# Four edits to a fused two-layer kernel: feed-forward weights loaded in the layer ahead, held-back expert loads, a reordered first tap in the scan, and another order of the scan's last projection

## The reference

```python
x = x + 0.5 * experts(layernorm(x))       # 8 experts, best 2 per token: silu(x@w1[e]) * (x@w3[e]) @ w2[e]
x = x + attention(layernorm(x))           # 32 heads of width 8, rotary positions
x = x + 0.5 * experts(layernorm(x))       # the same weights again
x = x + 0.5 * sparse_ffn(layernorm(x))    # silu(x@gate) * (x@up), best 2 of every 4 kept, @ down
x = x + state_space_scan(layernorm(x))    # 32 heads of 128: conv of 4 taps, silu, chunked scan, gate, norm, @ out_proj
x = x + 0.5 * sparse_ffn(layernorm(x))    # the same weights again
```

## Time and profile before

| | |
|---|---|
| three runs | 1654.58, 1649.94, 1653.99 us; median 1653.99 |
| profiled execution | 1655.48 us; span 1653.7 us, so 1.8 us lie around it |
| PE busy | 1437.4 us (87%), mean granted clock 0.939 |
| DVE / ACT / POOL busy | 1139.2 (69%) / 878.2 (53%) / 497.1 us (30%) |
| first expert layer | from 10.8 us |
| second expert layer | from 607.0 us |
| first feed-forward | from 775.7 us |
| scan heads | 980 to 1547 us |
| second feed-forward | 1548.6 to 1647 us |

### The profile page before, as it was taken

One profiled execution on the slowest core, in us unless ns is written; L12 is line 12 of the kernel. 1 busy time (PEld: TensorE's weight loads), 2 busy tenths in 40 slices (PEclk: granted clock), 3 DMA queues, 4 the chain that ended last, 5 costly groups with the idle time before them and its releaser, 6 DMA issues. The chain is left out here.

```text
span 1653.7 us, 25033 instructions
## 1 busy us (share of the span) xinstructions
PE 1437.4 (87%) x7896; PEld 1056.5 (64%) x7896; DVE 1139.2 (69%) x2026; ACT 878.2 (53%) x1238; POOL 497.1 (30%) x407
## 2 busy tenths in 40 slices
PE   3999489999999966994997968899999999998697
PEld 3788343333333345883786757788887887887586
DVE  5622599989989847332775756777776777867475
ACT  2422227767767744322434765667575665755332
POOL 1444210000000113542001114655645556564100
PEclk9999759999999977997997998999999999999899
DMA  8532211111111028334001103222322222221200
GB/s 296 146 52 46 58 31 21 23 25 20 27 28 27 5 96 286 52 52 120 2 0 40 42 25 91 83 90 90 96 77 85 77 96 90 84 90 39 77 1 26
DMA packets 83030, 112.06 MB, mean 68 GB/s; under 512 B 11905, under 2 KB 60801, under 8 KB 82913
## 3 DMA queue, kind: packets, MB, share of 16 engines
q1 hardware_dynamic: 73152, 96.05, 19.5%
q0 software_dynamic: 9376, 14.16, 4.8%
q10 hardware_dynamic: 384, 0.39, 0.1%
HBM read 89.99 MB, written 11.93 MB: 62 GB/s over the span
## 5 line engine op out<-in xcount | busy, mean ns | idle before, releaser
L962 DVE TENSOR_REDUCE attn_max_chunks<-attn_scores 128x1 f32<-128x512 f32 x488 | 305.4, 684 | 30.7 <-PE attn_scores L1213 25.2
L1124 ACT ACTIVATE attn_probs<-attn_scoresT 128x1024 f32<-128x1024 f32 x256 | 248.2, 1022 | 118.8 <-PE attn_scoresT L1229 118.6
L1213 PE MATMUL attn_scores<-attn_k_picks,attn_q_group 64*128 64x512 f32 x488 | 188.5, 466 | 14.5 <-DVE attn_max_chunks L962 6.0
L1213 PEld LDWEIGHTS attn_scores<-attn_k_picks,attn_q_group 64*128 64x128 f32 x488 | 85.7, 191 | 178.5 <-DVE attn_max_chunks L962 170.4
L1644 DVE SCALAR_TENSOR_TENSOR ssm_scan_x<-ssm_scan_proj,ssm_w_conv,ssm_scan_x 128x1023 f32<-128x1023 f32 (+2 forms) x96 | 123.1, 1282 | 84.1 <-ACT ssm_scan_x L1639 78.4
L1229 PE MATMUL attn_scoresT<-attn_q_group,attn_k_picks 64*128 64x512 f32 x512 | 153.9, 438 | 3.3 <-ACT attn_probs L1124 3.3
L1241 PE MATMUL attn_o<-attn_probs,attn_v_group 128*32 128x512 f32 x1024 | 139.2, 616 | 0.4 <-ACT attn_probs L1124 0.3
L62 PE MATMUL ssm_scan_proj<-ssm_xnT_hi,ssm_w_in_hi 128*128 128x512 f32 x256 | 111.0, 434 | 27.8 <-DVE ssm_scan_x L1644 22.5
L293 POOL DMA_INDIRECT moe_sums<-moe_xn,moe_token x46 | 77.7, 1690 | 128.4 <-DVE moe_xn L430 122.6
L2481 PE MATMUL ssm_scan_out<-ssm_scan_w_out,ssm_scan_v 128*128 128x256 f32 x480 | 110.7, 384 | 4.6 <-POOL ssm_scan_w_out L2186 4.4
L481 ACT ACTIVATE moe_xnT<-moe_gate 128x512 f32<-128x512 f32 x46 | 27.5, 597 | 153.6 <-PE moe_gate L64 153.6
(11 more groups left out here) (355 smaller groups left out, 3400.5 us busy)
## 6 DMA issues: line engine op xcount, KB each, us to landing
ssm_cum_all<-ssm_cums SPq DMA_DIRECT2D x32, 512.0 KB, 3.7
ssm_scan_exp_cum<-ssm_cums SPq DMA_DIRECT2D x32, 512.0 KB, 3.7
moe_w_gate_lo<-in_moe_w SPq DMA_DIRECT2D x16, 512.0 KB, 11.2
moe_w_up_lo<-in_moe_w SPq DMA_DIRECT2D x16, 512.0 KB, 11.1
moe_w_down<-in_moe_w SPq DMA_DIRECT2D x16, 512.0 KB, 11.1
ssm_w_in<-in_in_w SPq DMA_DIRECT2D x64, 128.0 KB, 2.6
ssm_scan_w_out<-in_out_w SPq DMA_DIRECT2D x8, 512.0 KB, 3.8
moe_sums<-main_residual SPq DMA_DIRECT2D x2, 1024.0 KB, 5.6
```

The source lines that it names most:

```text
L962: return nc.vector.tensor_reduce(rmaxc[:, half, place:place + 1], chunk_bank(g, n), AX_X, ALU.max).then_inc(reduced, 1)
L1124: nc.scalar.activation(probs[s % 2][:, 2 * pair:2 * pair + 2, :], st_ps[pair][:], ACT.Exp, scale=SCALE).then_inc(exp_done, 1)
L1213: nc.tensor.matmul(chunk_bank(g, n), qs[b][head_rows(j), t * P:(t + 1) * P], kz[b][head_rows(j), j % 2, c * BANK:(c + 1) * BANK], start=Tr ...
```

## The change

Four edits. (1) A buffer `ffn.room` of 32 KB a partition lives from the second expert layer to the end. In that layer it is `w_down`; when the last `down` product is done, SP loads the feed-forward's gate and up weights into it and waits for them, and only then waits for the scatter-adds and reloads `xres`. In the scan it holds `cT` and `cum_all`, and behind the last `cgrow` SP loads the same weights again. `sparse_ffn_layer` no longer loads them; ACT casts the first half of gate ahead of the first tokens, DVE subtracts for the first half of gate and the second of up, POOL for the other two. (2) In both expert layers SP holds back the loads of experts 4 to 7 until the first gather has landed; the casts of expert 0 come ahead of the router's tanh on ACT and its first subtraction ahead of the router on DVE; the others follow the first `low_x`; gate and up wait for their own parts, `down` for its own transfer. (3) In the scan ACT makes `tap(n+1)` before `square(n-1)`. (4) The last `w_out` goes into the buffer of `grow`, so that its load waits for `cgrow` alone; PE projects the first three heads of two pairs ahead of the last head's v, then adds the fourth, and `norm_sums` writes to the bank of y.

```diff
+SPLIT_AHEAD = 2
+LOAD_AHEAD = 4
...
+    def load(self, sync, loaded):
+        for n in self.src:
+            for k in range(KD):
+                sync.dma_start(self.raw[n][:, k, :], self.src[n][k * P:(k + 1) * P, :]).then_inc(loaded, 16)
+        sync.wait_ge(loaded, 2 * KD * 16)
...
             for e in range(EXPERTS):
+                if e == LOAD_AHEAD:
+                    sync.wait_ge(gathered[0], 16)
                 for name, src in (("gate", w1), ("up", w3)):
                     sync.dma_start(f32(w_lo[name][:, e * KD:(e + 1) * KD, :]), src[e].rearrange("(k p) n -> p k n", p=P)
                                    ).then_inc(expert_loaded[e], 16)
                 sync.dma_start(w_dn[:, e * KI:(e + 1) * KI, :], w2[e].rearrange("(k p) n -> p k n", p=P)
-                               ).then_inc(expert_loaded[e], 16)
+                               ).then_inc(down_loaded[e], 16)
+            if ffn is not None:
+                sync.wait_ge(q["out_done"], ITEMS)
+                ffn.load(sync, ffn_loaded)
             sync.wait_ge(summed, 16 * ITEMS)
...
+            def split_weights(e, n, name):
+
+                own = slice(e * KD, (e + 1) * KD)
+                dve.wait_ge(q["w_hi_done"], 2 * e + n + 1)
+                nc.vector.tensor_tensor(w_lo[name][:, own, :], f32(w_lo[name][:, own, :]), f32(w_hi[name][:, own, :]),
+                                        ALU.subtract).then_inc(q["w_lo_done"], 1)
+
+            split_weights(0, 0, "gate")
...
-            for e in range(SPLIT_AHEAD):
-                split_weights(e)
             low_x(0)
+            split_weights(0, 1, "up")
+            for e in range(1, SPLIT_AHEAD):
+                split_weights(e, 0, "gate")
+                split_weights(e, 1, "up")
             for i in range(ITEMS):
...
+            high_weights(0)
             act.wait_ge(q["logits_done"], 1)
...
-            for e in range(SPLIT_AHEAD):
+            for e in range(1, SPLIT_AHEAD):
                 high_weights(e)
...
             for i in range(ITEMS):
                 if i < EXPERTS:
-                    pe.wait_ge(expert_loaded[i], 48)
-                    pe.wait_ge(q["w_lo_done"], 2 * (i + 1))
+                    pe.wait_ge(q["w_lo_done"], 2 * i + 1)
                 gate(i, e)
                 if i:
                     turn_h(i - 1)
                 if i + 1 < ITEMS:
                     turn_x(i + 1)
+                if i < EXPERTS:
+                    pe.wait_ge(q["w_lo_done"], 2 * (i + 1))
                 up(i, e)
                 if i:
+                    if i <= EXPERTS:
+                        pe.wait_ge(down_loaded[i - 1], 16)
                     down(i - 1, e_before)
...
         def _(pool):
-            for n, c in w_parts:
-                if n == "gate":
-                    split_low(pool, nc.gpsimd, n, c)
+            split_low(pool, nc.gpsimd, "up", 0)
+            split_low(pool, nc.gpsimd, "gate", 1)
 
...
             normalize(0)
             normalize(1)
+            split_low(dve, nc.vector, "gate", 0)
             x_low(0)
-            split_low(dve, nc.vector, "up", 0)
             split_low(dve, nc.vector, "up", 1)
...
+            split(*w_parts[0])
             x_high(0)
-            for n, c in w_parts:
+            for n, c in w_parts[1:]:
                 split(n, c)
...
+        w_out_last = grow[:].rearrange("p (j d) -> p j d", j=NORM_HEADS)
...
             def load_out(gw):
-                if after(gw, 1):
+                if is_at(gw, G - 1):
+                    sync.wait_ge(q["cgrow_done"], HM)
+                elif after(gw, 1):
                     sync.wait_ge(q["out_mm"], PAIRS * gw)
                 src = out_w[bass.ds(gw * NORM_HEADS * PD, NORM_HEADS * PD), :].rearrange("(j p) d -> p j d", p=P)
-                sync.dma_start(w_out[:], src).then_inc(w_out_in, 16)
+                sync.dma_start(w_out_last if is_at(gw, G - 1) else w_out[:], src).then_inc(w_out_in, 16)
...
             load_out(G - 1)
+            sync.wait_ge(q["cgrow_done"], HM)
+            ffn.load(sync, ffn_loaded)
...
 
-            def ahead(n, j, gw, norm_of=None):
+            def ahead(n, j, gw, norm_of=None, square_of=None):
                 tap(n, j)
+                if square_of is not None:
+                    square(*square_of)
                 grow_of(n)
...
             def body(n, j, gw):
+                passed = (n - 1, (j - 1) % G, gw - (j % NORM_HEADS == 0)) if after(n, 1) else None
                 if not is_at(n, LAST):
-                    ahead(n + 1, j + 1, gw + (j % NORM_HEADS == NORM_HEADS - 1), gw - 1 if j % NORM_HEADS == 0 and after(n, 1) else None)
-                square(n, j, gw)
+                    ahead(n + 1, j + 1, gw + (j % NORM_HEADS == NORM_HEADS - 1),
+                          gw - 1 if j % NORM_HEADS == 0 and after(n, 1) else None, passed)
+                else:
+                    square(*passed)
...
             def norm_sums(gw):
                 pe.wait_ge(q["summed"], SUMS * (gw + 1))
-                if after(gw, 1):
+                if is_at(gw, G - 1):
+                    pe.wait_ge(q["y_done"], HM)
+                elif after(gw, 1):
...
+            def project_last(p, heads_of):
+
+                first, end = heads_of[0] == 0, heads_of[-1] == NORM_HEADS - 1
+                for m in range(2):
+                    cols = slice((2 * p + m) * P, (2 * p + m + 1) * P)
+                    for jn in heads_of:
+                        last = nc.tensor.matmul(tail_ps[p][:, m, :], v[:, v_row((G - 1) % 2 * NORM_HEADS + jn), cols], w_out_last[:, jn, :],
+                                                start=(first and m == 0 and jn == 0), stop=(end and jn == NORM_HEADS - 1),
+                                                skip_group_check=True)
+                if end:
+                    last.then_inc(q["out_mm"], 1)
...
             heads(pe, body)
-            for p in range(PAIRS):
-                for m in range(2):
-                    project_out(G - 1, (G - 1) % 2, p, m, tail_ps[p])
-                if p == 0:
-                    norm_sums(G - 1)
+            pe.wait_ge(q["w_out_scaled"], G)
+            pe.wait_ge(q["v_done"], LAST)
+            pe.wait_ge(q["added"], PAIRS * (G - 1))
+            for p in range(2):
+                project_last(p, range(NORM_HEADS - 1))
+            pe.wait_ge(q["v_done"], HM)
+            for p in range(2):
+                project_last(p, (NORM_HEADS - 1,))
+            norm_sums(G - 1)
+            for p in range(2, PAIRS):
+                project_last(p, range(NORM_HEADS))
```

96 lines of the change are left out of this document (47 added, 49 removed).

## The result

The changed kernel takes **1629.64 us** (median of 1630.38, 1628.90, 1631.11 and 1627.83), where the kernel before has 1654.28 over four runs: ratio 0.984, with a 95% interval of 0.981 to 0.987. The profiled execution has a span of 1628.6 us against 1653.7. The forecast was 1629.2, in a range of 1618 to 1642.

What follows compares the result with a forecast made beforehand. Layers follow one another, each with its own limit; in the scan loop PE is full but for two short waits. Seven parts, 2.9 + 0.6 + 0.8 + 5.6 + 5.5 + 5.9 + 3.5 = 24.8 us, off 1653.99: 1629.2 us, range 1618 to 1642.

Steps and rivals of the forecast that it cites:

- First expert layer: First gather lands in 2.7 instead of 6.2 us, less 0.6 us for held-back loads: 2.9 us gained, bounds 0 and 3.5.
- Second expert layer: Gather gains 3.5 us, tanh and router come 2.4 us late, 0.5 off for loads: 0.6 us gained, bounds -2.4 and 1.9.
- First feed-forward: Front gains 3.2 us, residual reload comes 2.4 us late: net 0.8 us gained, bounds -0.8 and 1.6.
- POOL beside DVE: Feed-forward fronts: POOL's last subtraction stays 3.05 us beside DVE's; extreme case, POOL standing still, ends 2.1 us later, sum 20.6.
- The rival that the gather gains nothing: Expert layers: something other than the load backlog held the gather; gain 17.8 us in all, 1636 us; chance 0.10.
- Scan, first heads: First four scan heads: taps 0.96 us earlier each, 3.9 us, plus 1.7 us of clock: 5.6 us, bounds 3.9 and 10.7.
- My third rival: First four scan heads: the clock stays up in all, 5.1 us more gained, 1624 us; chance 0.13.
- Scan, loop: PE's two waits vanish, 0.6 us in each of 9 heads, 0.1 at the exit: 5.5 us, bounds 0 and 11.5.
- The rival that put POOL's `xend` as the next limit: Scan loop: PE's waits only displaced, loop gains 0, first heads lose 3.2 us; 16.1 in all, 1638 us; chance 0.15.
- Scan, end: Last `w_out` loads early and PE goes on without waiting for scaled weights: 5.9 us gained, bounds 4.4 and 6.0.
- Second feed-forward: Weights already there, load gone from the path, products start sooner: 3.5 us gained, bounds 2.5 and 4.4.
- Slower, by POOL's squares behind the tap: Scan: POOL loses 0.6 us a head waiting for later squares, 19 us if POOL limits; near 1660 us; chance 0.04.

Runs made afterwards that it cites:

- the tap alone: Kernel before the change with one edit, ACT making the first tap of head n+1 ahead of the square of head n-1: 1634.1 us, ratio 0.988.

## Why the prediction was right, step by step

- **First expert layer, 2.9 us.** The gather was right (3.4 us at its place). The term that failed is "I take off 0.6 us because the held-back 6 MB now run beside the first scatter-adds and the fifth gather": that cost 3.5 us, all that was won, and 2 to 3.5 us in the six profiles with this layer. The 1.05 us of the table came from elsewhere. I had the slow landing of 6.2 us in hand, and did not apply it to the gather that the held-back loads would meet.
- **Second expert layer, 0.6 us.** Casts and table load ahead of the tanh: 2.4 forecast, 2.2 measured. The gather won 3.5. The same term for the loads, 0.5, was 2.4, so the layer lost 1.1 us to its last scatter-add. In the other profiles the term is 1.4 to 4.4, and the experiment without held-back loads does not show that they are all of it.
- **First feed-forward, 0.8 us.** The reload came 3.6 us later, not 2.4 (2.7 to 3.7 in the eight profiles with this load; it took 9.4 us beside the scatter-adds, not 8.2), and the front won 2.5 us, not 3.2. Together -1.2, below the lower bound of -0.8. Counted whole, from the last `down` to the end of the layer, it is 0.8 us lost.
- **POOL beside DVE.** I kept 3.05 us for POOL's last part, wrongly: it took 3.83 us in the first feed-forward and 3.91 in the second. In the earlier trace rows the two overlap by 1.03 us only; POOL lost nothing there, but DVE's part took 2.87 us where it takes 2.03 alone, and I compared only POOL's two. After the change they overlap by 2.78 us, POOL loses 0.77 and DVE 1.60, together 2.37, nearly the time of the overlap. That POOL shares its SBUF interfaces with VectorE and contends with its instructions of two SBUF inputs is what the Trainium skill says ("GPSIMD Engine Reference", "Specifications", table of engine properties). The runs agree, in the size just given and not in the 2.1 us of my extreme case.
- **The rival that the gather gains nothing** fell: the first gather landed in 6.2 and 6.4 us beside the backlog before and in 2.8 without it after, in both expert layers; the fifth did so the other way round, 2.7 and 2.9 us before and 5.7 and 5.0 after. The Trainium skill's round-robin between queues by packet ("DMA: Bandwidth & Descriptors", "Queues, rings and completion order", on arbitration) is neither shown nor refuted here. That it makes a gather independent of the backlog was my conclusion from it, and these landings don't bear it out.
- **Scan, first heads, 5.6 us**, measured 6.9, and 5.4 to 9.4 over the 13 profiles with the tap first, as the clock fell. The tap was right to 0.1 us a head. For the clock I counted the first of the four, whose wait I saw fall from 1.90 to 0.94; it stayed at 1.90, for no square stands ahead of that tap. The clock came back in two of the others, 1.6 us each. My third rival, that it comes back in all four, was right in no profile.
- **Scan, loop, 5.5 us**, measured 11.2, nearly its upper bound. The 0.6 for a head was 0.74, but not from the two waits that I added up. The stop for the taps gave 0.57 us with a row of 0.30. The wait for the states, 0.45 us, stands in two of the twelve heads alone and did not vanish: it is 0.28 after the change, and `from_states` comes 0.17 to 0.19 us earlier behind the gate products, in a head without the row too. The larger part is that "three of these gain nothing" and "0.1 at the exit" did not hold: the last heads of a four, the back edge and the exit gained 5.3 us, and more in the other profiles. The rival that put POOL's `xend` as the next limit, and this part at nothing, fell. It has a share only in the last head of a four, where PE's wait for it grew from 1.27 to 1.80 us.
- **Scan, end, 5.9 us**, measured 5.7, or 6.4 against the tap alone. The sum was right, the split was not: load and order were 4.4 and 1.5 in it, and are 3.5 and 3.0, and the load's part holds 1.4 us of slow clock that the sum did not name.
- **Second feed-forward, 3.5 us**, measured 3.1; POOL's last part, 0.86 us longer than I had it, is more than the difference.
- **Slower, by POOL's squares behind the tap.** POOL waits 0.85 us for the square in the head shown above, as feared, and the head is 0.74 us shorter all the same.

In short: the seven mechanisms were there, the gather's only at its own place. The two terms for what moved loads do to others were some five times too small in this profile, the term for the scan's loop was half of its size or less, and these errors happened to cancel. That the total fits to half a microsecond is luck.

## What to carry to other kernels

When a load is held back, list what else is issued while it runs in its new place, and give each of these the slow latency that the trace already shows; the cure here was to issue the small urgent transfer one step earlier. A wait at the end of a block holds up the whole next block (18.8 us from the last `down` to the block, and 15.4 with the wait moved); put it at the first reader. And a fair sum can hide two wrong terms: compare stage by stage before a mechanism is called confirmed.

## What the runs showed of the hardware

- PE's granted clock in the 4 us after a wait of 2.52 us was 1.00 in one head and 0.60 after one of 2.51 in another of the same execution; one head's difference is 1.6 us. After a wait of 2.73 us it was 1.00, after one of 2.11 us 0.67.
- DVE and POOL, both subtracting with two SBUF inputs, slow each other by nearly the time that they overlap (2.37 us lost in 2.78).
- PE lost 0.57 us at a stop whose row shows 0.30 us idle.
- An indirect gather landed in 2.7 to 3.4 us ahead of the held-back loads and in 4.7 to 7.8 beside them; the first scatter-add of a layer landed in 4.5 to 4.7 us with nothing held back and in 6.7 to 7.8 beside the held-back loads.
- Code that no edit touched varied by 5 us in attention and 4 us in `prepare` between profiles.
